# Both ends of the first attention and the last layer's stages in another order, in a four-layer network on one core

## Reference

```
x = x + L0_attn(L0_cond(x, cond_8))        # cond: x @ (W_base + 2*sum_e w_e Bs_e As_e).T + b, per sample
  L0_attn: q, k, v = 16 heads of 8, times mod = cos(phase)*amplitude
           scores * cos(2 pi (i-j)/S); w = softmax; w = (w + roll(w, 1)) / sqrt(2); (w @ v) @ Wo
x = x + L0_ffn(L0_cond2(x, cond_8))
  L0_cond2: masked_w = weight * mask; w_bot[b] = sum_g y[b,g] masked_w[g]; x @ w_bot[b].T + bias
  L0_ffn:   act_qdq(x): scale = max|x| over the whole tensor / 32767, round, times scale
            up, gate products, sigmoid, product, each quantised so; down product
...
x = x + L3_attn(L3_cond(...))              # causal, 16 heads
x = x + L3_ffn(L3_cond2(x, cond_8))
  L3_cond2: as L0_cond
  L3_ffn:   h = silu(x@w1.T*s1) * (x@w2.T*s2); h = gelu(h@h1.T*sh1); h = gelu(h@h2.T*sh2); h@w3.T*s3
```

## Time and profile before

| | |
|---|---|
| median of 3 runs | 1317.19 us (1313.71 to 1318.36) |
| the profiled execution | 1312.5 us |
| its span, first to last instruction | 1310.6 us |
| PE busy | 1209.5 us, 92% |
| DVE, ACT, POOL busy | 824.5 us, 647.9 us, 275.4 us |
| mean granted TensorE clock | 0.987 of full speed |

### The profile page before, as it was taken

The page is one execution under the profiler, slowest core; times in us unless marked ns, Lnnn a source line. Parts: engine busy times, 40 slices in busy tenths (PEclk is TensorE's granted clock), DMA queues, the critical chain, the costliest instruction groups (busy, mean ns, idle before and its releaser), DMA issues.

```text
span 1310.6 us, 28370 instructions
## 1 busy us (share of the span) xinstructions
PE 1209.5 (92%) x10425; PEld 970.9 (74%) x10425; DVE 824.5 (63%) x1740; ACT 647.9 (49%) x1327; POOL 275.4 (21%) x356
## 2 busy tenths in 40 slices
PE   8899867889999899999999999899999999988999
PEld 5667423568888799877788887499889876656777
DVE  7988697654565667566776465566564477754342
ACT  4678584354334244444444444244434367655553
POOL 7677001200023134220000023134230032100000
PEclk9999988999999999999999999999999999999999
DMA  9000202310503132105034002032111000000000
GB/s 327 11 2 2 81 1 94 123 65 1 217 13 109 48 102 66 33 16 217 1 145 182 1 15 62 10 114 71 36 55 48 1 3 3 3 2 1 1 17 17
DMA packets 43332, 75.87 MB, mean 58 GB/s; under 512 B 3896, under 2 KB 34240, under 8 KB 42304
## 3 DMA queue, kind: packets, MB, share of 16 engines
q1 hardware_dynamic: 39104, 65.66, 13.8%
q0 software_dynamic: 4096, 8.40, 2.2%
HBM read 59.75 MB, written 14.29 MB: 56 GB/s over the span
## 4 chain that ended last, share of the span: by engine, by line
PE 73%; DVE 16%; ACT 6%; issue 3%; DVEq 1%; DMA 0%; POOL 0%; ACTq 0%; POOLq 0%
PE banks L1987 8%; PE banks L1998 7%; PE banks L1983 7%; PE banks L2042 5%; PE banks L1974 4%; PE banks L2052 3%; PE banks L1712 3%; PE banks L1717 3%; PE banks L1719 3%; PE banks L1718 3%; PE banks L1967 2%; PE banks L1969 2%; PE banks L1968 2%; DVE SC L2336 2%; PE banks L1850 2%
## 5 line engine op out<-in xcount | busy, mean ns | idle before, releaser
L2249 ACT ACTIVATE SC<-banks 128x512 f32<-128x512 f32 x192 | 114.4, 596 | 224.4 <-PE banks L1983 126.8
L2336 DVE SCALAR_TENSOR_TENSOR SC<-banks,SM,SC 128x512 f32<-128x512 f32 x128 | 95.8, 748 | 121.9 <-PE banks L1987 103.3
L1998 PE MATMUL banks<-A,SC 128*128 x1024 | 137.1, 277 | 7.8 <-DVE SC L2336 7.1
L1987 PE MATMUL banks<-X,SC 128*128 128x128 f32 x1024 | 136.9, 277 | 4.2 <-DVE SC L2609 3.6
L1983 PEld LDWEIGHTS banks<-X,SC 128*128 128x128 f32 x1024 | 126.1, 192 | 19.5 <-issue 12.5
L1983 PE MATMUL banks<-X,SC 128*128 128x128 f32 x1024 | 136.1, 276 | 4.4 <-ACT SC L2233 3.2
L1998 PEld LDWEIGHTS banks<-A,SC 128*128 128x128 f32 x1024 | 125.3, 192 | 17.4 <-issue 16.5
L1987 PEld LDWEIGHTS banks<-X,SC 128*128 128x128 f32 x1024 | 124.5, 192 | 6.7 <-DVE SC L2609 6.4
L2042 PE MATMUL banks<-A 128*128 128x128 f32 x736 | 100.4, 280 | 11.8 <-DVE A L2759 6.2
L2042 PEld LDWEIGHTS banks<-A 128*128 128x128 f32 x736 | 90.1, 193 | 16.6 <-ACT A L2274 9.2
L2233 ACT ACTIVATE SC<-A 128x512 f32 x128 | 80.6, 630 | 28.3 <-PE banks L1987 22.9
(11 more groups left out here) (348 smaller groups left out, 2528.3 us busy)
## 6 DMA issues: line engine op xcount, KB each, us to landing
A<-in_moe SPq DMA_DIRECT2D x36, 768.0 KB, 10.0
A<-xs SPq DMA_DIRECT2D x20, 256.0 KB, 3.5
ys<-A SPq DMA_DIRECT2D x20, 256.0 KB, 2.4
BW<-in_l1f SPq DMA_DIRECT2D x2, 2048.0 KB, 7.4
BW<-in_l2f SPq DMA_DIRECT2D x1, 3456.0 KB, 11.8
BW<-in_l1c SPq DMA_DIRECT2D x1, 3072.0 KB, 16.2
BW<-in_l3f SPq DMA_DIRECT2D x1, 2816.0 KB, 9.6
A<-in_l1c SPq DMA_DIRECT2D x1, 2560.0 KB, 8.5
```

Source lines behind the costliest of these rows:

```text
L1987: m = e.matmul(at["pu"].ap[:, cut(q)], wx[:, cut(4 + q)], x, start=True, stop=True)
L1998: m = e.matmul(o, at["h"].ap[:, cut(q)], W[:, bass.ds(r + (1024 + 128 * q), 128)], start=k == 0 and q == 0, stop=k == 1 and q == 3)
L2249: e.activation(at["h"].ap, at["pg"].ap, ACT.Gelu_apprx_tanh).then_inc(at["gelu"][0], 1)
L2336: return e.scalar_tensor_tensor(out=o, in0=a, scalar=s, in1=b, op0=o1, op1=o2)
```

## The change

1. **Start.** `warm(8)` becomes `warm(5)`, and the `warm(2)` between product and add goes. Chunk 1's `cw_scale` and `cw` are issued right behind those of chunk 0, its `cw_add` after `mod`; they leave `todo`. `wmask` waits for chunk 0's `v_shift`. `spread` moves from `first_half(0)` to `second_half(0)`, behind the second softmax.
2. **End of attention 0.** For the last half, DVE copies the first transposed bank and ACT the second. The row sums of the last group go to a bank of their own, two parts with each half. Chunk 3's cond2 is folded: `wfold` (PE, one product of 512 columns) forms Wo times w_bot, `cond2_x` applies w_bot to X before the attention's output is added, `fold_out` (ACT) copies both, `cond2_o` (PE) applies the folded weight to the heads' output and DVE adds it to Y. The add into X follows later, between POOL's maximum and the scale. Y's first chunk is quantised by DVE alone. `y_max(2)` moves behind `cond2_o`. `keep_on(4)` becomes `keep_on(6)`. The constants grow by o0T (128 columns).
3. **Last layer.** cond of chunk n is an item of two stages and a second item; the first stages of chunks 0 to 2 and `l3_y` of chunks 0 and 1 stand among the attention's head halves (behind numbers 12, 15, 17, 20, 23, 25 and 28). `silu_next`, an ACT instruction on one column, stands behind the last ones. `turns` changes, and in `l3_up` silu and multiply of block m+1 go before the halves of block m. The halves wait for x3 of chunk 3, which `l3_y` no longer does.

```diff
-        warm(8, True)
+        (scale1,), (product1, add1), _ = (it[1] for it in cond0[1])
+        warm(5, True)
         scale()
+        scale1()
         product()
-        warm(2)
+        product1()
         add()
         last()
...
         at["m"], t_mod = tick("prep_dve"), tick("mod")
+        add1()
...
+                    w.wait_ge(*at["after"])          # wmask: after=sig["shift", 0]
...
             def first_half(p):
                 if p:
-                    parts[p - 1, 1][1]()
+                    parts[p - 1, 1][1](by=("vec" if p == 16 else "act", "act"))
...
+                if p == 16:
+                    fold_begin()
+                    fold_end()
...
             def second_half(p):
                 if p < 16:
                     parts[p, 1][0]()
+                    if p == 0:
+                        parts["spread"]()
                     parts[p, 0][1]()
...
                 if p == 16:
-                    for n in range(3):
-                        y_max(n)
+                    y_max(0)
+                    y_max(1)
...
                 if p == 16:
+                    cond2_o(chunk[3]["o"], chunk[3]["to"])
                     parts["out", 3]()
+                    y_max(2)
...
+        def fold_begin():
+            at = step("wfold", wbot=sig["wb", 12], pa=RA.take())
+            at["mm"] = tick("c2_mm")
+            bt = step("cond2_x", pa=RA.take())
+            bt["mm"] = tick("c2_mm")
+            fold.update(w=at, x=bt)
...
-        items.append(([("x0", 3)], [lambda: cond2(3, RA)], ("y0b", 3)))
...
-        keep_on(4)
+        keep_on(6)
...
-        scl, inv, t = scale_of(mx, 4, sig["ymax"])
+        scl, inv, t = scale_of(mx, 4, sig["ymax"], (), sig["x0_later"])
...
-            turns = [(n, 0) for n in (0, 1)] + [(n, k) for k in (1, 2) for n in (0, 1)]
-            turns += [(2, 0), (0, 3), (1, 3), (2, 1), (0, 4), (1, 4), (3, 0), (3, 1), (2, 2), (3, 2), (2, 3), (3, 3),
-                      (2, 4), (3, 4)]
...
-        seq = (items + flat(seq[12:]) + flat(mix(m3, f2, m4, shared_items())) + at3 + cond_items("y3b", 3, "x3")
-               + l3_ffn_items())
+        beside3 = {12: cond3[0][0], 15: cond3[0][1], 17: ffn3[0][0], 20: cond3[1][0], 23: cond3[1][1], 25: ffn3[1][0],
+                   28: cond3[2][0]}
...
+        nothing = ([], [lambda: None], None)
+        end3 += [nothing, cond3[3][0], ([], [silu_next], None), nothing, cond3[2][1]]
+        turns = [(0, 1), None, (1, 1), (0, 2), (1, 2), (2, 0), (3, 0), (0, 3), (1, 3), (0, 4), (2, 1), (1, 4), (3, 1),
+                 (2, 2), (3, 2), (2, 3), (3, 3), (2, 4), (3, 4)]
...
                 elif kind == "l3_up":
                     over(at["h"])
-                    for m in range(4):
...
+                    for m in range(5):
+                        if m < 4:
+                            over(at["r"][m])
+                            w.wait_ge(*at["mm"][2 * m])
+                            e.activation(at["r"][m].ap, at["pg"][m].ap, ACT.Silu, scale=c("s1")[:, m:m + 1]).then_inc(at["silu"][m][0], 1)
+                        if m > 0:
+                            k = m - 1
+                            w.wait_ge(*at["after"])
+                            w.wait_ge(*at["mul"][k])
+                            e.activation(at["h"].ap[:, 512 * k:512 * k + 512], at["r"][k].ap, ACT.Copy).then_inc(at["hi"][k][0], 1)
```

More of the change, by code:

```diff
@@ L306, in add @@
                     ring.give(at["pa"], at["sum"])
-                def all3(scale=scale, product=product, add=add):
-                    scale()
-                    product()
-                    add()
                 def s1(n=n, st=st, ring=ring):
@@ L321, in cond_items @@
                 if src_key:
-                    items.append(([(src_key, n)], [all3, s1], (key, n)))
+                    items.append((([], [scale, lambda product=product, add=add: (product(), add())], None), ([(src_key, n)], [s1], (key, n))))
                 else:
@@ L552, in s_norm @@
                                 st["o"] = RO.take()
-                            at = step("norm", j=j, pc=st["pc", j], pv=u["pv"], o=st["o"], rr=RR.take())
+                            at = step("norm", j=j, pc=st["pc", j], ps=st.get(("ps", j)), pv=u["pv"], o=st["o"], rr=RR.take())
                             at["rcp"], at["t"] = tick("att_vec"), tick("att_vec")
@@ L557, in s_norm @@
                             (RC if i else RC0).give(st["pc", j], at["t"])
+                            if at["ps"] is not None:
+                                RA.give(at["ps"], at["rcp"])
                         def s_soft(s_max=s_max, s_exp=s_exp):
@@ L697, in masked @@
                 sig["wmask"] = tick("wmask")
-                step("wmask")
+                step("wmask", after=sig["shift", 0])
             steps = [masked]
@@ L743, in cond2, with fold_end, cond2_o @@
             ring.give(at["pa"], at["y"])
+        fold = {}
+        def fold_begin():
[4 more added lines that the diff above has]
+            fold.update(w=at, x=bt)
+        def fold_end():
+            at, bt = fold["w"], fold["x"]
+            ct = step("fold_out", w=at, x=bt, to=RWB.take(), yfree=sig["Yfree", 3])
+            at["t"], bt["t"] = tick("c2_fold"), tick("c2_y")
+            RA.give(at["pa"], at["t"])
+            RA.give(bt["pa"], bt["t"])
+            fold["to"] = ct["to"]
+        def cond2_o(o, to):
+            at = step("cond2_o", w=fold["to"], ready=fold["w"]["t"], yx=fold["x"]["t"], o=o, to=to, pa=RA.take())
+            at["mm"] = sig["wbot_over"] = tick("c2_mm")
+            at["y"] = sig["y0b", 3] = tick("c2_add")
+            RA.give(at["pa"], at["y"])
         def y_max(n):
@@ L1827, in _ @@
                                          at["p"][-1].ap[:, cut(4 * x + h)], start=g == 0, stop=g == 3)
-                    for g in range(4 if at["half"] else 0):
+                    own = at["ps"] is not None
+                    sums = at["ps"].ap[:, 0:128] if own else pc[:, 128:256]
+                    if own:
+                        over(at["ps"])
+                    for g in range(2 * at["half"], 2 * at["half"] + 2) if own else range(4 if at["half"] else 0):
                         for h in range(4):
-                            m = e.matmul(pc[32 * h:32 * h + 32, 128:256], c("sumw")[:, 32 * g:32 * g + 32],
+                            m = e.matmul(sums[32 * h:32 * h + 32, :], c("sumw")[:, 32 * g:32 * g + 32],
                                          at["p"][g // 2].ap[:, cut(4 * (g % 2) + h)], start=g == 0, stop=g == 3)
@@ L1870, in _ @@
                         m = e.matmul(at["pa"].ap[:, cut(j)], WBOT[:, b, :], X[:, b, :], start=True, stop=True)
+                    m.then_inc(at["mm"][0], 1)
+                elif kind == "wfold":
+                    over(at["pa"])
+                    w.wait_ge(*loaded["cst2"])
+                    w.wait_ge(*at["wbot"])
+                    e.matmul(v4(at["pa"].ap), c("o0T"), WBOT[:, 12:16, :], start=True, stop=True).then_inc(at["mm"][0], 1)
+                elif kind == "cond2_x":
+                    over(at["pa"])
+                    for j in range(4):
+                        m = e.matmul(at["pa"].ap[:, cut(j)], WBOT[:, 12 + j, :], X[:, 12 + j, :], start=True, stop=True)
+                    m.then_inc(at["mm"][0], 1)
+                elif kind == "cond2_o":
+                    over(at["pa"])
+                    w.wait_ge(*at["ready"])
+                    w.wait_ge(*at["to"])
+                    for j in range(4):
+                        m = e.matmul(at["pa"].ap[:, cut(j)], at["w"].ap[:, cut(j)], at["o"].ap[:, cut(j)], start=True, stop=True)
                     m.then_inc(at["mm"][0], 1)
@@ L2201, in _ @@
                     e.activation(ch(Y, at["n"]), v4(at["pb"].ap), ACT.Identity).then_inc(at["t"][0], 1)
+                elif kind == "silu_next":
+                    e.activation(at["to"], c("s1")[:, 0:1], ACT.Silu)
                 elif kind == "decay":
@@ L2447, in _ @@
                     e.tensor_tensor(v4(at["s"].ap[:, 0:4 * k]), pa[0], bc_last(m[:, 0:4], k), ALU.add).then_inc(at["sub"][0], 1)
+                elif kind == "turn" and "vec" in at["by"]:
+                    over(at["p"])
+                    for x, pb in enumerate(at["pb"]):
+                        if at["by"][x] == "vec":
+                            w.wait_ge(*at["tr"][x])
+                            e.tensor_copy(at["p"].ap[:, 512 * x:512 * x + 512], pb.ap).then_inc(at["t"][x][0], 1)
                 elif kind == "norm":
@@ L2452, in _ @@
                     w.wait_ge(*at["pv"])
-                    e.reciprocal(at["rr"].ap, pc[:, 128:256]).then_inc(at["rcp"][0], 1)
+                    sums = pc[:, 128:256] if at["ps"] is None else at["ps"].ap[:, 0:128]
+                    e.reciprocal(at["rr"].ap, sums).then_inc(at["rcp"][0], 1)
                     w.wait_ge(*at["rcp"])
                     e.tensor_tensor(at["o"].ap[:, cut(j)], pc[:, 0:128], at["rr"].ap, ALU.mult).then_inc(at["t"][0], 1)
```

(7 more changed lines are left out.)

133 lines of the change are left out of this document (83 added, 50 removed).

## The result

The changed kernel takes 1322.32 us (median; 1318.67 to 1323.80), the kernel before 1317.26 beside it: ratio 1.0036, 95% interval 1.0026 to 1.0046. It is slower by a third of a per cent. My 1300.0 us was wrong by 22 us and the time is outside the range. The profiled execution has a span of 1320.2 us; that of before, 1310.6, belongs to an execution 4.7 us under its median, so 9.6 us of difference between the two traces shows 5 of difference between the kernels. I come back to that.

What follows compares the result with a forecast made beforehand. PE and DVE were taken to alternate in the first 50 us, and PE to bound the last layer wherever it has work. Gains 4.1 + 1.0 + 12.1 = 17.2 us off 1317.2 gave 1300.0 us, range 1296 to 1304.

Steps and rivals of the forecast that it cites:

- bounds 0 and 1.35 each, 9.5 together; I take 0.15 each, 1 us: Last attention: cost of seven items among the heads, each making a round without scores; 1 us lost in all.
- part 3: Last layer, attention drain and feed-forward block: 12.1 us won, bounds 3.5 and 14.5.
- rival A: Last attention: scoreless rounds stall PE 1.35 us seven times, or cond's adds hold DVE 2 us four times; 1308.5 us, chance 0.13.
- The block: Last layer's feed-forward: 10.7 us of gaps, laid to ACT's order in `l3_up`, shrink to 1.3 us.
- Rival D: Last layer: DVE still paces `l3_up` near 2 us, only the drain is won; about 1309 us, chance 0.05.
- The drain: Last layer, between attention and feed-forward: 4.55 us of PE idle time falls to 0.8.
- Part 1: Start of the kernel: 4.1 us won by the second group's scores, bounds 2 and 5.5.
- The shift: Start: with `wmask` behind it, `v_shift`'s 4-column DVE instruction no longer waits on POOL; 1.7 us won.
- values and scale: Start: `v_out` and chunk 1's scale move into times when DVE idles; 1.5 us won.
- The warm-up: Start: fewer warm products let the first real ones begin earlier; 0.9 us won, bounds -1 (low clock) and 1.2.
- Rival B: Start: the lead is lost, POOL holding up another DVE instruction or the clock being late; 1304.1 us, chance 0.12.
- Part 2: End of attention 0: 1.0 us won, `keep_on` finishing later than the quantising; bounds -0.7 and 2.0.

Runs made afterwards that it cites:

- e6: e4 with `l3_y` of chunks 0 and 1 moved from beside the last attention to behind it; 1301.39 us, ratio 0.9915 to the kernel before.
- e7: The changed kernel with every stage moved from beside the last attention to behind it, products still pipelined; 1297.24 us, ratio 0.9893 to the kernel before.
- e5: e3 plus seven empty rounds, without instructions or scores, in the last attention; 1314.55 us, ratio 1.0019 to the kernel before.
- e4: The changed kernel with conditioning scales a round earlier and DVE's adds behind the softmax in the last attention; 1314.44 us, ratio 0.9986 to the kernel before.
- e3: The kernel before plus the start and attention 0 edits and the new `l3_up` loop, last-layer items in old order; 1311.68 us, ratio 0.9973.
- e8: e7 with the old, longer warm-up restored; 1299.38 us, ratio 0.9896 to the kernel before.
- e10: The kernel before with only the edits at the end of attention 0; 1313.06 us, ratio 0.9997.
- e11: e7 with `keep_on(3)` instead of `keep_on(6)`, six products fewer; 1296.73 us, ratio 0.9872 to the kernel before.
- e1: The changed kernel with the last layer as before, so only the start and end of attention 0 edited; 1315.38 us, ratio 0.9998 to the kernel before.
- e9: The kernel before with only the start edits; 1309.19 us, ratio 0.9973.
- e12: e7 with layer 0 as before, without the edits to the start and the end of attention 0; 1299.68 us, ratio 0.9900 to the kernel before.
- e2: The kernel before with only the last-layer edits, layer 0 as before; 1321.73 us, ratio 1.0050.

## Why the prediction was wrong

**What failed** is the term "bounds 0 and 1.35 each, 9.5 together; I take 0.15 each, 1 us", and what the sum left out beside it. The attention grew by 23.3 us. 5.5 of it is work that was done later before (busy PE 92.4 in e6 against 86.9 in e7: 1.3 for 32 values products that fall into the stretch in e5 too, 4.2 for the conditioning). The other 17.8 (12.8 more idle, 5.0 at the lower clock) stand against my 1.0. In the table's sums the whole of part 3 lost 5.9 us where I had 12.1 won: 18.0 of the 22 us. The prediction had named PE idle before the transposes as a sign of being wrong, and that is what the rows show. The step from the changed kernel to e7 divides the loss, by the table's sums:

- 6.2 us from DVE's adds (247.4 to 241.2, e4). That is rival A's second half, which I priced at 2 us four times.
- 6.3 us from `l3_y` beside the attention (241.2 to 234.9, e6). I priced its two stages as two rounds and their work at nothing. They have no product, so PE gets an empty round each, 2.1 us at e5's rate. The other 4.2 would be its instructions on ACT and DVE; e4's trace shows them waiting for each other with a softmax behind, but no run has measured that share by itself.
- 5.2 us from the five rounds that the conditioning fills (234.9 to 229.7, e7), 1.04 each. PE's 4.2 us of work in them fill the rounds, but taking that work out of the drain made the part behind the last scores only 3.7 us shorter (12.9 against 16.6).

Seven empty rounds cost 7.4 us (e5), 1.06 each: seven times what I took, within my bound of 1.35. "ACT and DVE each have a fifth to a quarter of their time free there" was the reason, and it does not hold. The free time lies in the waits of a loop in which PE is at 10.00 of 10, so a head that comes a round late is not made up. Rival A had the mechanism and too small a price (8.5 us): its two halves come to 13.6 (7.4 and 6.2), and it left out `l3_y`'s instructions. The lower clock behind the pauses is in these sums.

**The block.** Predicted 9.4 us won (10.7 less 1.3), measured 7.5. I gave all 10.7 to ACT's order in `l3_up`. By my own rows six rounds of 2.05 us instead of 1.36 are only 4.1 us; most of the rest are the pauses ahead of a stage's first product, which the loop does not touch. It does what I said (rounds of 1.37 us in e3) and brings 2.2, or 3.8 but for the fall of the clock; the rest of the order brings the other 5.3. So the sum for the block was near for a reason that was half wrong. Rival D had DVE holding the rounds near 2 us, and e3 refutes that.

**The drain.** Predicted 4.55 us of idle time going to 0.8; it went to 1.33. Right.

**Part 1.** The shift 1.7 predicted and 1.7 measured, values and scale 1.5 and 1.56. The warm-up, 0.9 predicted, was -0.6, inside its bounds of -1 and 1.2: the products began at 3.75 us as worked out and ran at the lower clock. The Trainium skill ("TensorE: Matmul & The Clock Gate", What's actually happening) has the low clock as the default and activity as what ends it. The trace after agrees, with four products at 0.95 us each, and is nearer to my lower bound than to my term. But the -0.6 is that of one profile. In the nine with this start the first q product begins between 8.38 and 10.53 us (9.36 after, 8.75 before), so the term was anything from 0.4 to -1.8, and e8 has slow products behind the longer warm-up too. Altogether 2.65 us instead of 4.1 at the second group, 2.2 at the attention's end. Rival B had both halves of its reason in small. The clock was late; and chunk 1's shift, which now runs beside POOL (30.73 to 32.01), took 1.43 us instead of 0.68. Behind it PE's pause before the next scores is 0.74 us longer. After, then before:

```profile
31.12 1.43 DVE L2499 TENSOR_TENSOR A<-Y 128x508 f32<-128x508 f32 x1
...
36.22 1.15 PE L1847 MATMUL banks<-A 32*128 32x256 f32 x16 [2.39 <-DVE A L2540]
```

```profile
33.76 0.68 DVE L2406 TENSOR_TENSOR A<-Y 128x508 f32<-128x508 f32 x1
...
38.12 1.15 PE L1789 MATMUL banks<-A 32*128 32x256 f32 x16 [1.65 <-DVE A L2447]
```

That the one causes the other is read from the rows and not tested by a run.

**Part 2.** Predicted 1.0 us with `keep_on` as the later one; 1.2 in e10, and e11 shows that it was the later one. Right.

In time, parts 1 and 2 together are worth 0.3 us [-0.9, 1.6] in e1, and part 1 alone 3.6 [1.2, 5.9] in e9. The two hardly agree; the first feed-forward product comes 1.8 us earlier in e1's profile and 3.0 in that of the kernel after. What the whole program keeps of that stays open.

**The profile of before as a base.** Between the first feed-forward product and the last attention nothing was edited, yet it took 917.4 us before and 924.0 after; the other kernels had 915.3 to 923.4, in no order that follows the edits. They differ in steps of a few us at different places. That is as large as half of what I wanted to predict, and explains why the two traces are 9.6 us apart and the medians 5.

## What to carry to other kernels

Work moved beside a stage in which the bound engine has no free time is only free if it needs no round of its own, and if none of its instructions waits on another engine while the stage's own work is queued behind it: price both from the loop's queue, not from the free share of an engine. Put the empty rounds in first, without the work: one run tells if there is slack. And try the plain order beside the interleaved one: here the loop, the turns and the order in the drain held all of the last layer's gain, and without the interleaving the changed kernel was 1.4% faster.

## What the runs showed of the hardware

The clock column is no guide in the first microseconds. In the kernel after it says 1.00 while the four products of `cond` take 0.95 us each, twice their time at 2.4 GHz:

```profile
4.00:5.00 1.00, 1.00 (x2) 0.48 (x3) 0.01 (x1) 0.00 (x0) 1.00 (x1) 1.00 0.95 303
```

The products behind the warm-up reached full speed at a time that varied from profile to profile. With sixteen warm products ahead the first two real ones took 1.02 us (e10, e12), 1.17 (before), 1.32 (e2) and 1.91 (e8). With ten, the first four took from 2.51 us (e7) to 3.78 (after, e1) in nine profiles, and in none were all four at full speed; they also start 0.4 to 1.1 us sooner. In e1 the eight products behind them still took 1.88 us instead of 1.05, until 9.6 us. So the longer warm-up may help and guarantees nothing. I had treated the clock there as a consequence of its length alone.

From 30 to 50 us the granted clock is 0.91 with PE busy 17.1 of 20 us after, and 1.00 with 16.5 before. Finer windows show one fall to 0.50, from about 38 to 41 us, and the slow products are themselves part of the fuller stretch:

```profile
39.00:40.00 1.00, 1.00 (x6) 1.00 (x5) 0.97 (x2) 0.00 (x0) 0.00 (x0) 0.50 0.00 0
```

Ahead of it stands PE's pause of 2.39 us. In nine profiles a pause of 2.39 to 2.45 us goes before such a fall; in the four with the start of before the pause is 1.65 to 1.66 us and the clock stays at 1.00. But e1 has a pause of 2.41 us at the same place and keeps 1.00, so the pause alone does not decide; what does was not found. The pauses of 1.88 us (e3) and 1.72 us (before) in the feed-forward block are another such pair, the first with a fall behind it and the second without.
